# Cross-attention in a decoder layer: a new order of tasks, another bank for the maxima's transposes, and the keys' stack by way of HBM

## What is computed

```python
q = w8a8_linear(x, wq, bq)              # x quantised by row to integers, wq by row
k = cond @ wk.T + bk
v = cond @ wv.T + bv
scores = einsum('bhnd,bhld->bhnl', q, k) / sqrt(D) + mask
o = einsum('bhnl,bhld->bhnd', softmax(scores), v)
return w8a8_linear(o, wo, bo)           # o quantised by row again
```

## Time and profile before

| what | value |
|---|---|
| median of 3 runs | 4096.11 us (4090.36 to 4101.38) |
| the profiled execution's own time | 4115.7 us |
| its span, first to last instruction | 4114.0 us |
| PE busy | 3691.4 us (90%) |
| DVE busy | 2596.5 us (63%) |
| ACT busy | 1596.1 us (39%) |
| POOL busy | 648.8 us (16%) |
| mean granted TensorE clock | 0.942 |
| moved by DMA | 256.97 MB |

### The profile page before, as it was taken

The page is one execution under the profiler, slowest core; times in us unless marked ns, Lnnn a source line. Parts: engine busy times, 40 slices in busy tenths (PEclk is TensorE's granted clock), DMA queues, the critical chain, the costliest instruction groups (busy, mean ns, idle before and its releaser), DMA issues. The chain is left out here.

```text
span 4114.0 us, 95372 instructions
## 1 busy us (share of the span) xinstructions
PE 3691.4 (90%) x34364; PEld 2671.0 (65%) x34364; DVE 2596.5 (63%) x6225; ACT 1596.1 (39%) x2842; POOL 648.8 (16%) x784
## 2 busy tenths in 40 slices
PE   7999999994899989989898998899899859999998
PEld 6988999993556655655655555565565636666665
DVE  4444444444677767767777777677777756666665
ACT  3222223221344544444444444444445433332322
POOL 0000000003011111101111011111111103332222
PEclk9999999997899999999999999899999979999999
DMA  2000000003546454654646555364554520000000
GB/s 94 13 13 12 9 7 8 12 9 76 95 90 106 90 103 84 109 94 82 108 80 111 91 97 101 73 113 89 95 102 93 93 60 5 13 12 17 15 12 13
DMA packets 121819, 256.97 MB, mean 62 GB/s; under 512 B 18564, under 2 KB 99276, under 8 KB 118364
## 3 DMA queue, kind: packets, MB, share of 16 engines
q1 hardware_dynamic: 113136, 243.95, 31.5%
q10 hardware_dynamic: 8300, 7.69, 0.7%
HBM read 99.79 MB, written 9.83 MB: 27 GB/s over the span
## 5 line engine op out<-in xcount | busy, mean ns | idle before, releaser
L1391 DVE CUSTOM_DVE_ANT_0 ca_rowmax<-ca_rowmax,ca_msk 100x1024 f32<-100x1024 f32 (+1 forms) x1024 | 929.2, 921 | 383.6 <-PE ca_rowmax L1159 377.1
L1097 ACT ACTIVATE ca_prob<-ca_unit 128x800 f32<-128x800 f32 x640 | 534.6, 835 | 558.7 <-PE ca_unit L1283 558.6
L1159 PE MATMUL ca_rowmax<-ca_ks,ca_qs 96*100 96x512 bf16 (+1 forms) x1536 | 518.6, 408 | 81.0 <-DMA ca_ks<-ca_ks 47.6
L1283 PEld LDWEIGHTS ca_unit<-ca_qs,ca_ks 99*128 99x128 bf16 (+1 forms) x6144 | 356.0, 100 | 212.2 <-issue 124.8
L1002 POOL TENSOR_TENSOR ca_key_part<-ca_key_rest,ca_key_part 128x512 bf16<-128x512 f32 (+1 forms) x192 | 211.5, 1102 | 1680.3 <-ACT ca_key_part L1064 1680.3
L1246 PE MATMUL ca_acc<-ca_prob,ca_vaug 128*17 128x100 f32 x12288 | 444.6, 258 | 21.1 <-issue 20.8
L1283 PE MATMUL ca_unit<-ca_qs,ca_ks 99*128 99x100 bf16 (+1 forms) x6144 | 439.4, 212 | 24.1 <-issue 15.3
L1141 PE MATMUL ca_ring<-ca_wvT,ca_ctxT 128*128 128x256 f32 (+1 forms) x1536 | 418.2, 419 | 0.9 <-ACT ca_qs L1075 0.6
L1141 PEld LDWEIGHTS ca_ring<-ca_wvT,ca_ctxT 128*128 128x128 f32 (+1 forms) x1536 | 314.9, 207 | 79.7 <-issue 17.8
L1132 PE MATMUL ca_ring<-ca_ctxT,ca_wkT 128*128 128x512 f32 (+1 forms) x768 | 346.1, 573 | 2.3 <-ACT ca_ctxT L1048 2.3
L1159 PEld LDWEIGHTS ca_rowmax<-ca_ks,ca_qs 96*100 96x100 bf16 x1536 | 154.7, 128 | 243.8 <-issue 173.1
(11 more groups left out here) (260 smaller groups left out, 6598.3 us busy)
## 6 DMA issues: line engine op xcount, KB each, us to landing
ca_ks<-ca_key_part SPq DMA_DIRECT2D x768, 90.2 KB, 4.1
ca_ks<-ca_ks SPq DMA_DIRECT2D x64, 722.0 KB, 5.7
ca_ctx<-in_ctx SPq DMA_DIRECT2D x32, 1408.0 KB
ca_ks<-ca_ks SPq DMA_DIRECT2D x64, 361.0 KB, 8.9
ca_msk<-in_mask_BxSxS_ff SPq DMA_DIRECT2D x32, 564.1 KB
sa_w_stage<-in_L_attn_w_qkv SPq DMA_DIRECT2D x12, 512.0 KB, 5.4
sa_x_in<-in_x ACTq DMA_DIRECT2D x8, 400.0 KB
sa_x_res<-in_x SPq DMA_DIRECT2D x8, 400.0 KB
```

Of the source, the lines that this page charges most:

```text
L1097: act.activation(prob[:, s, :], unit[:, :, 0:QUAD * N], ACT.Exp).then_inc(bc.freed[0], 1)
L1159: last = pe.matmul(rowmax[0:N, s0:s1], qs[0:STACK, par, h, :], ks[0:STACK, par, h, s0:s1], start=True, stop=True)
L1283: return pe.matmul(unit[0:rows(t0 + k), k, j * N:(j + 1) * N], ks[:, par, h, keys(k)], qs[:, par, h, :], start=(j == 0), stop=True, skip_g ...
L1391: dve.tensor_tensor_reduce(rowmax[0:N, s0:s1], rowmax[0:N, s0:s1], msk[:, par, s0:s1], 1.0, -3.0e38, ALU.add, ALU.max, top[:, bank, h:h + ...
```

## The change

Five edits, all in `cross_attention`:
1. The table of tasks is written anew. The key tasks end in slot 7 where they ended in slot 9, most value tasks come a slot or two earlier, the rest moves around them.
2. `mr` leaves `unit` for the third bank of `rowmax`, which it shares with ml.
3. The keys are stacked by way of a scratch tensor in HBM: three writes of 128 rows (722 KB each), one for each part, then for each half of the heads six reads of 16 rows (361.0 KB each), one for each term. All reads wait for all three writes. SP's order is: the three writes, the six reads of the first half, the context load, the six reads of the second half, and the rest as before.
4. The values' eviction goes from VectorE to ScalarE and leaves out the bias; the bias is added once to the output of the batch (softmax weights sum to one), one more VectorE step of 100x256 in `eo`.
5. The last pair of tiles has one exponential over both full tiles; rows past the 36 valid ones are not read afterwards.

```diff
--- before.py
+++ after.py
@@ -709,30 +709,30 @@
...
         0: [("mh", 6), ("ct", 0, 0), ("ct", 0, 1), ("ml", 6)],
-        1: [("eo",), ("kp", 0, 0)],
-        2: [("mh", 7), ("kp", 0, 1), ("km", 0, 0)],
-        3: [("ml", 7), ("ct", 1, 0), ("ct", 1, 1), ("ex",), ("km", 0, 1)],
-        4: [("mh", 8), ("kp", 1, 0), ("ml", 8), ("ey",)],
-        5: [("mr", 1), ("mh", 9), ("kp", 1, 1), ("km", 1, 0)],
-        6: [("ml", 9), ("ct", 2, 0), ("ct", 2, 1), ("km", 1, 1), ("ez",)],
-        7: [("mh", 10), ("kp", 2, 0), ("ml", 10)],
-        8: [("mh", 11), ("kp", 2, 1), ("km", 2, 0)],
-        9: [("ml", 11), ("vp", 0), ("km", 2, 1)],
-        10: [("mh", 12), ("qq",), ("ml", 12)],
-        11: [("mr", 2), ("qx",), ("mh", 13), ("vp", 1), ("qp",)],
-        12: [("ml", 13)],
-        13: [("mh", 14), ("vp", 2), ("ml", 14), ("qs", 0)],
-        14: [("mh", 15), ("qs", 1), ("ma",)],
-        15: [("ml", 15), ("vp", 3)],
-        16: [("mh", 0), ("ml", 0)],
-        17: [("mr", 3), ("mh", 1), ("vp", 4), ("mf",)],
-        18: [("ml", 1)],
-        19: [("mh", 2), ("ml", 2)],
-        20: [("mh", 3), ("vp", 5)],
-        21: [("ml", 3)],
-        22: [("mh", 4), ("ml", 4)],
-        23: [("mr", 0), ("mh", 5)],
-        24: [("ml", 5)],
+        1: [("eo",), ("kp", 0, 0), ("mh", 7)],
+        2: [("ml", 7), ("kp", 0, 1), ("km", 0, 0), ("ct", 1, 0), ("ct", 1, 1)],
+        3: [("ex",), ("mh", 8), ("kp", 1, 0), ("km", 0, 1)],
+        4: [("ml", 8), ("ey",), ("kp", 1, 1), ("km", 1, 0), ("ct", 2, 0), ("ct", 2, 1)],
+        5: [("mr", 1), ("mh", 9), ("kp", 2, 0), ("km", 1, 1)],
+        6: [("ml", 9), ("kp", 2, 1), ("km", 2, 0), ("mh", 10), ("ez",)],
+        7: [("ml", 10), ("vp", 0), ("km", 2, 1)],
+        8: [("mh", 11), ("ml", 11), ("qq",)],
+        9: [("vp", 1), ("mh", 12)],
+        10: [("ml", 12), ("qx",), ("mh", 13)],
+        11: [("mr", 2), ("vp", 2), ("qp",), ("ml", 13)],
+        12: [("mh", 14), ("ml", 14)],
+        13: [("vp", 3), ("mh", 15)],
+        14: [("ml", 15), ("qs", 0), ("qs", 1), ("ma",)],
+        15: [("vp", 4)],
+        16: [("mr", 3), ("mh", 0), ("ml", 0)],
+        17: [("mh", 1), ("mf",)],
+        18: [("ml", 1), ("mh", 2)],
+        19: [("ml", 2), ("mh", 3)],
+        20: [("ml", 3), ("vp", 5)],
+        21: [("mh", 4), ("ml", 4)],
+        22: [("mr", 0), ("mh", 5)],
+        23: [("ml", 5)],
+        24: [],
     }
@@ -753,8 +753,8 @@
...
     ring_order = [t for t in timeline if t[0] in ("ct", "kp", "vp", "qx", "qp", "qs", "mf")]
-    cur_order = [t for t in timeline if t[0] in ("u", "mr")]
-    top_order = [t for t in timeline if t[0] in ("mh", "ml", "eo", "ex", "ey")]
+    cur_order = [t for t in timeline if t[0] == "u"]
+    top_order = [t for t in timeline if t[0] in ("mh", "ml", "mr", "eo", "ex", "ey")]
@@ -770,7 +770,7 @@
...
         bc = Banks(nc, sems, "ca_cur", cur_order, lambda t: 0, lag={t: 1 - batch_of(t) for t in cur_order})
-        bm = Banks(nc, sems, "ca_top", top_order, lambda t: int(t[0] == "ml"),
+        bm = Banks(nc, sems, "ca_top", top_order, lambda t: int(t[0] in ("ml", "mr")),
                    lag={t: 1 - batch_of(t) for t in top_order})
@@ -793,6 +793,7 @@
...
         key_rest = sb("key_rest", [P, 2, THIRD * TL])
+        key_rows = nc.dram_tensor("key_rows_scratch", [2, PARTS, P, C * S], BF16, kind="Internal").ap()
         ks = sb("ks", [FULL, 2, H, S], BF16)
@@ -833,7 +834,7 @@
...
         hi_out, parts_out, mid_out = sem("hi_out"), sem("parts_out"), sem("mid_out")
-        placed = [sem(f"placed{k}") for k in range(H // HALF)]
+        placed = sem("placed")
         stacked = [sem(f"stacked{k}") for k in range(H // HALF)]
@@ -850,10 +851,9 @@
...
-        O_STEPS = 8
-        O_HALF = 6
-        PLACED = 16 * HALF // C * PARTS
-        STACKED = 16 * 2
+        O_STEPS = 9
+        O_HALF = 7
+        STACKED = 16 * TERMS
@@ -868,29 +868,21 @@
...
-            def stack(b, par):
-
-                def put(half, parts):
-                    for part in parts:
-
-                        standing_wait(sp, (hi_out, mid_out, parts_out)[part], 6 * (b + 1), sp_passed)
-                        for n in range(half * HALF // C, (half + 1) * HALF // C):
-                            sp.dma_start(ks[DH * part:DH * (part + 1), par, n * C:(n + 1) * C, :],
-                                         key_part[DH * n:DH * (n + 1), part, :, :]).then_inc(placed[half], 16)
-
-                def repeat(half):
-                    heads = slice(half * HALF, (half + 1) * HALF)
-                    standing_wait(sp, placed[half], PLACED * (b + 1), sp_passed)
-                    sp.dma_start(ks[3 * DH:5 * DH, par, heads, :], ks[0:2 * DH, par, heads, :])\
+            def keep(b, par):
+
+                for part in range(PARTS):
+                    standing_wait(sp, (hi_out, mid_out, parts_out)[part], 6 * (b + 1), sp_passed)
+                    sp.dma_start(key_rows[par, part], key_part[:, part, :, :].rearrange("p c s -> p (c s)"))\
+                        .then_inc(placed, 16)
+
+            def stack(b, par, half):
+
+                heads = slice(half * HALF, (half + 1) * HALF)
+                n0, n1 = half * HALF // C, (half + 1) * HALF // C
+                for term, part in enumerate((0, 1, 2, 0, 1, 0)):
+                    sp.dma_start(ks[DH * term:DH * (term + 1), par, heads, :].rearrange("d (n c) s -> d n (c s)", c=C),
+                                 key_rows[par, part].rearrange("(n d) x -> d n x", d=DH)[:, n0:n1, :])\
                         .then_inc(stacked[half], 16)
-                    sp.dma_start(ks[5 * DH:6 * DH, par, heads, :], ks[0:DH, par, heads, :])\
-                        .then_inc(stacked[half], 16)
-
-                put(0, (0, 1, 2))
-                put(1, (0,))
-                repeat(0)
-                put(1, (1, 2))
-                repeat(1)
@@ -902,12 +894,15 @@
...
                 first = isinstance(b, int) and b < 2
+                keep(b, par)
+                standing_wait(sp, placed, 16 * PARTS * (b + 1), sp_passed)
+                stack(b, par, 0)
                 if more:
...
                     load_ctx(b + 1)
-                stack(b, par)
+                stack(b, par, 1)
                 if more:
@@ -1052,8 +1047,7 @@
...
                     if (k, c) == (0, 0) and not (isinstance(b, int) and b == 0):
-                        for k in range(H // HALF):
-                            act.wait_ge(placed[k], PLACED * b)
+                        act.wait_ge(placed, 16 * PARTS * b)
                     act.activation(key_part[:, 0, c, s], ring[bn.bank(task)][:, 0:w], ACT.Identity,
@@ -1063,6 +1057,20 @@
...
                         .then_inc(mid_out, 1)
+                elif task[0] == "vp":
+                    bank = bn.bank(task)
+                    bn.wait_full(act, task, b)
+                    t = 2 * task[1]
+
+                    def v_out(r, n0, n1):
+                        return act.activation(
+                            vaug[0:r, par, t + n0:t + n1, :, 0:DH],
+                            ring[bank][0:r, n0 * D:n1 * D].rearrange("p (t h d) -> p t h d", t=n1 - n0, h=H), ACT.Copy)
+                    if rows(t + 1) == TL:
+                        v_out(TL, 0, 2).then_inc(bn.freed[bank], 1)
+                    else:
+                        v_out(TL, 0, 1)
+                        v_out(last_rows, 1, 2).then_inc(bn.freed[bank], 1)
                 elif task[0] == "qx":
@@ -1077,11 +1085,10 @@
...
                     h0 = task[1] * QUAD
-                    bank = bc.bank(task)
-                    bc.wait_full(act, task, b)
+                    bm.wait_full(act, task, b)
                     act.activation(qs[STACK:FULL, par, h0:h0 + QUAD, :].rearrange("p h n -> p (h n)"),
-                                   unit[STACK:FULL, 0, :].bitcast(BF16)[:, 0:QUAD * N], ACT.Copy)\
-                        .then_inc(bc.freed[bank], 1)
+                                   rowmax[STACK:FULL, 2 * 512:3 * 512].bitcast(BF16)[:, 0:QUAD * N], ACT.Copy)\
+                        .then_inc(bm.freed[bm.bank(task)], 1)
                 elif task[0] == "ex":
@@ -1091,14 +1098,10 @@
...
                     return
-                t, s = 2 * (p % PER_QUAD), slice(2 * (p % 2), 2 * (p % 2) + 2)
+
                 bc.wait_full(act, ("u", p), b)
-                if rows(t + 1) == TL:
-                    act.activation(prob[:, s, :], unit[:, :, 0:QUAD * N], ACT.Exp).then_inc(bc.freed[0], 1)
-                else:
-                    act.activation(prob[:, s.start, :], unit[:, 0, 0:QUAD * N], ACT.Exp)
-                    act.activation(prob[0:rows(t + 1), s.start + 1, :], unit[0:rows(t + 1), 1, 0:QUAD * N],
-                                   ACT.Exp).then_inc(bc.freed[0], 1)
+                act.activation(prob[:, 2 * (p % 2):2 * (p % 2) + 2, :], unit[:, :, 0:QUAD * N], ACT.Exp)\
+                    .then_inc(bc.freed[0], 1)
@@ -1161,13 +1164,13 @@
...
                 if kind == "mr":
-                    g, bank = task[1], bc.bank(task)
```

(26 more changed lines are left out.)

## The result

The changed kernel takes 4682.15 us (median of 4 runs, 4660.93 to 4691.17) against 4098.74 for the kernel before, run beside it: 1.1418 times, interval 1.1372 to 1.1464. The forecast, 4300 with a range to 4370, had the sign and missed the size: +583 us instead of +201.

A forecast was written before the change was run, and what follows sets the result against it. TensorE, 90% busy and in order, was taken to bound the kernel, beside the keys' chain. A turn of 53.1 + 6.0 + 15.5 + 3.4 = 78.0 us against 71.7, over 31 turns +195, gave about 4300 us, range 4055 to 4370.

The forecast's parts named there:

- The sign: Whole kernel: slower than before, chance 0.70, against faster 0.22 and same 0.08.
- VectorE's new waits: TensorE behind VectorE or a shared bank in the new order: five waits, 6.35 us a turn in sum.
- the first sign: At the row maxima (mh 0): the wait for the DMA grows to some 6 us in every turn.
- The reads' rate: Key reads from HBM into 16 partitions: 114 GB/s taken, so 19.5 us for a half of 2.22 MB.
- rival 1: Key reads not held back by 16 partitions: over 164 GB/s, turn 70.3 us, about 4055 us; chance 0.22.
- The writes: Key writes to HBM, 739,328 bytes each: 2.3 us taken, plus 2.5 us for issue and landing.
- rival 3: Slower than forecast: writes at the lower bound land 10 us later, turn 80 us or more, 4370 us; chance 0.10.
- a half's reads as one wait before mh 0: First half of the keys lands at 59.1 us, 6.0 us after TensorE is ready at 53.1.
- The clock: TensorE's clock falls behind the wait for the keys: 3.4 us a turn, mean clock near 0.93.
- The sum: One turn: 53.1 + 6.0 + 15.5 + 3.4 = 78.0 us against 71.7, +6.3.
- Rival 4: VectorE's new waits are the loss, keys arrive in time, two clock falls a turn: 75.4 us, 4215 us; chance 0.10.

The follow-up runs named there:

- path only: Kernel before plus only the keys' way through HBM (3 writes, 12 reads of 16 rows a batch), old order and banks: 4511.93 us, 1.1001 times.
- two in flight: Changed kernel with at most two of the 16-row key reads queued at once, same bytes and partitions: 4533.19 us, 1.1028 times.
- no path: Changed kernel with the keys stacked inside SBUF by the small copies of before: 4196.74 us, 1.0240 times.
- the idle reads: Kernel before plus four 361 KB HBM loads a turn into 16 unused partitions, nobody waiting: 4196.26 us, 1.0241 times; issued one at a time, 4119.99 us.

## Why the prediction was right and wrong

- **The sign: right, with the wrong wait behind it.** The loss was given to the keys' reads through 16 partitions, with VectorE's new waits beside them. The reads do carry it ("path only", +10%), but the first sign that I had named for it, a wait of some 6 us for the keys in every turn, didn't come: it was 7.5 us in 27 turns. The mean clock, 0.93 forecast, was 0.88.
- **VectorE's new waits: right in size.** Ct 1 1 2.77 (2.0 predicted), ct 2 1 1.58 (1.5), mh 8 0.62 (0.7), mh 13 0.86 (1.3), mr 0 1.16 just after the turn's end (0.85): 6.99 against 6.35. Net of what went away, "other" rises by 3.1 us a turn; the sum had 6.35 - 3.88 = 2.5.
- **The reads' rate: right, and rival 1 falls.** 116 and 120 GB/s against 114 taken, 164 needed for the rival. The Trainium skill, SBUF — State Buffer, "Door 1: The DMA port swizzle", gives about 109 for partitions 0 to 15; the prediction left open whether that holds for reads from HBM. The two stretches here lie 6 and 10% above it: near enough to hold as a guide, and the measurement decides. The 341 GB/s that the Trainium skill, DMA: Bandwidth & Descriptors, "Measured", has for 128 partitions was no guide to reads into 16.
- **The writes: right, or a little better.** 3.4 us from issue to landing, against 2.3 + 2.5 in the sum; the lower bound of rival 3 didn't occur.
- **The step that failed: a half's reads as one wait before mh 0.** I costed 19.5 us of full DMA engines at exactly what stands behind them on a semaphore, 6.0 us, and the context, query and mask loads at nothing. TensorE's own instructions come through the same engines, and no term was for them. The bare stops cost 9.5 us a turn more than before, and they swallow the wait that I predicted: 0.3 us. With two reads in flight it comes out at 6.3, the size of my 6.0 (partly luck, since paced reads are another chain). So a wait of that sort exists, under a larger stop.
- **The clock: mis-sized, a second failed term.** I let one fall of 3.4 us follow the keys' wait, as before, so nothing net. (The view of 1976 to 1983 us before has 7 us at 0.51 behind the wait, which is where such a figure comes from.) TensorE's busy time grew by 7.5 us a turn for the same work. "Path only" gives +4.3, two in flight +6.2, VectorE's waits alone ("no path") +0.8. It isn't only a consequence of the bare stops: two in flight has hardly any, its wait for the keys is the one I predicted, and its turn is still 86.3 us where my sum had 78.0. By subtraction, then, a wait grown from 1.3 to 6.3 us a turn costs some 5 us of clock that I had priced at nothing; no run has that wait by itself.
- **The sum.** Per turn: bare stops +9.5, slower products +7.5, other waits +3.1, keys -1.0, together 19.1 against 19.0 measured. Mine was +6.3. The difference of 12.7 a turn times 31 is 394 us, against a miss of 382. The 12.7 are 9.5 for the stops, 7.5 for the clock and 0.6 for VectorE's waits, less 4.9 for the keys' wait, which I had grow by 3.9 and which shrank by 1.0.
- **Rival 4** (VectorE's waits are the loss, 4215) described the change without its path, 4196.74; that this is near is partly luck, since it added a whole clock fall and "no path" shows 0.8 us of busy time. With the path it wasn't the case at hand.

What the runs show is that the stops come with queued reads from HBM into 16 partitions and go with the queue, and that in the changed kernel, "path only" and the idle reads every stop over 2 us ends just behind a packet of instructions, most often one that began late. That these packets are TensorE's own is inferred from this timing, from the rows' "issue" and from stops in the middle of a group of like products. It is open why five stores out of 16 partitions, nearly as long in the queues (12.3 us against 13.8), do no harm: direction, size of the pieces and place of the partitions were changed together, and twelve such stores did come with stops of 3.4 us a turn (of the 15 over 2 us, 7 end within 3 us of a packet, so some of them have another cause). The 70 us by which the two parts together cost more than each alone lie mostly in the clock: busy time grows by 4.3 and 0.8 us a turn alone and by 7.5 together, and the 2.4 over, times 31, are 74 us. Why it falls further together is open.
